# Second attention of a four-layer kernel: value packs in pairs, and one row-sum group added on DVE

## What is computed

```python
h, dh = 8, 32                                   # 8 heads of 32 channels, T = 2048
q, k, v = ...                                   # [b, h, t, dh], float32
attn = softmax(einsum('bhqd,bhkd->bhqk', q, k) * 256 ** -0.5)
attn_out = einsum('bhqk,bhkd->bqhd', attn, v)
# tokens e*512..(e+1)*512 keep only the first 256 >> e channels of attn_out:
out[:, sl, :m] = attn_out[:, sl, :m] @ o_w[:m, :m].T + o_b[:m]
```

## Time and profile before

| what | value |
|---|---|
| median of 3 executions | 5029.73 us (5026.91 to 5038.87) |
| the profiled execution | 5029.49 us |
| its span, first to last instruction | 5027.3 us, mean granted TensorE clock 0.944 |
| PE busy | 4622.3 us (92%) |
| DVE busy | 4207.0 us (84%) |
| ACT busy | 3361.4 us (67%) |
| POOL busy | 1333.6 us (27%) |

### The profile page before, as it was taken

The page is one execution under the profiler, slowest core; times in us unless marked ns, Lnnn a source line. Parts: engine busy times, 40 slices in busy tenths (PEclk is TensorE's granted clock), DMA queues, the critical chain, the costliest instruction groups (busy, mean ns, idle before and its releaser), DMA issues. The chain is left out here.

```text
span 5027.3 us, 89365 instructions
## 1 busy us (share of the span) xinstructions
PE 4622.3 (92%) x33659; PEld 2057.7 (41%) x33659; DVE 4207.0 (84%) x5551; ACT 3361.4 (67%) x6016; POOL 1333.6 (27%) x881
## 2 busy tenths in 40 slices
PE   6998775896999999999999999999998889999993
PEld 3333541563333333333333333333334445545532
DVE  6999650787999999999999999999994777777736
ACT  4888110231888888888888888888884426666663
POOL 2333210462000000000000000000001239999992
PEclk9999887996999999999999999999997769999996
DMA  5111569687333333344333333433314831323305
GB/s 188 56 55 42 186 232 394 198 271 159 43 55 50 49 49 49 50 55 55 53 49 49 49 49 54 55 55 49 49 20 153 289 86 46 82 60 79 74 5 170
DMA packets 408176, 479.48 MB, mean 95 GB/s; under 512 B 165056, under 2 KB 311264, under 8 KB 390848
## 3 DMA queue, kind: packets, MB, share of 16 engines
q1 hardware_dynamic: 394464, 455.41, 39.2%
q10 hardware_dynamic: 13280, 18.35, 1.1%
HBM read 315.71 MB, written 155.58 MB: 94 GB/s over the span
## 5 line engine op out<-in xcount | busy, mean ns | idle before, releaser
L763 DVE TENSOR_REDUCE at_NM<-at_MX 128x1 f32<-128x1024 f32 (+1 forms) x3008 | 3066.3, 1049 | 241.1 <-PE at_MX L611 216.2
L715 ACT ACTIVATE at_PB<-at_S 128x512 f32<-128x512 f32 x5056 | 2712.1, 597 | 628.3 <-PE at_S L638 503.7
L611 PE MATMUL at_MX<-at_KT,at_QT 48*128 48x512 f32 (+1 forms) x5056 | 1904.2, 454 | 60.6 <-DMA at_VS<-v 46.0
L638 PE MATMUL at_S<-at_QT,at_KT 50*128 50x512 f32 (+1 forms) x5056 | 1898.6, 441 | 8.4 <-ACT at_PB L715 6.0
L650 PE MATMUL at_AV<-at_PB,at_VS 128*32 128x256 f32 (+1 forms) x18304 | 1555.5, 414 | 0.9 <-ACT at_PB L715 0.9
L638 PEld LDWEIGHTS at_S<-at_QT,at_KT 50*128 50x128 f32 (+1 forms) x5056 | 804.8, 187 | 901.1 <-ACT at_PB L715 824.8
L611 PEld LDWEIGHTS at_MX<-at_KT,at_QT 48*128 48x128 f32 (+1 forms) x5056 | 795.8, 190 | 312.5 <-DVE at_NM L763 209.5
L650 PEld LDWEIGHTS at_AV<-at_PB,at_VS 128*32 128x32 f32 x18304 | 369.8, 108 | 820.9 <-ACT at_PB L715 752.0
L547 POOL CAST at_NMR<-at_NMF 16x128 fp32r<-16x128 f32 x79 | 22.1, 279 | 1837.5 <-ACT at_NMF L727 1837.5
L572 POOL TENSOR_TENSOR at_SUM<-at_SUM,at_PB 128x2048 f32<-128x2048 f32 x90 | 415.0, 4611 | 10.9
L913 PE MATMUL wkv_PQ<-wkv_XT,wkv_WT 128*128 128x512 f32 x768 | 340.5, 600 | 50.8 <-DVE wkv_DL L1036 34.2
(11 more groups left out here) (211 smaller groups left out, 3368.0 us busy)
## 6 DMA issues: line engine op xcount, KB each, us to landing
at_QT<-qk SPq DMA_DIRECT2D x402, 128.0 KB, 5.2
moe_W<-in_w SPq DMA_DIRECT2D x48, 1024.0 KB, 11.4
at_KT<-qk SPq DMA_DIRECT2D x384, 128.0 KB, 6.5
at_VS<-v SPq DMA_DIRECT2D x96, 256.0 KB, 9.0
at_KT<-qk SPq DMA_DIRECT2D x96, 256.0 KB, 6.3
qk<-r_HI SPq DMA_DIRECT2D x36, 512.0 KB, 4.2
qk<-r_LO SPq DMA_DIRECT2D x36, 512.0 KB, 5.2
ycat<-wkv_Y SPq DMA_DIRECT2D x32, 512.0 KB, 2.6
```

The lines of the kernel that those rows point to most:

```text
L611: ins = nc.tensor.matmul(MX[r][:, a, :], q_of(s)[h:h + NQ, b * P:(b + 1) * P], k_of(it, s, b * P // W)[h:h + NQ, (c + a) * W:(c + a + 1) * W],
L638: nc.tensor.matmul(SP_[item(it, s, "score", t)[1]][:, :], k_of(it, s, c)[h:h + NQ + 2, kb * P:(kb + 1) * P], q_of(s)[h:h + NQ + 2, c * W:( ...
L715: nc.scalar.activation(PB[:, t % NPB, :], SP_[r][:, :], ACT.Exp, scale=scale).then_inc(exp_done, 1)
L763: nc.vector.tensor_reduce(NM4[:, b, c:c + 1], MX[r][:, :, :].rearrange("p a n -> p (a n)"), AX_X, ALU.max, negate=True).then_inc(ring_got, 1)
```

## The change

Two edits in the second attention. First, the value pack of an even key block is moved to the step of the odd one behind it: `value_step(v)` uses `v | 1`, so the value packs of blocks 0 and 1 both stand after step 10, those of 2 and 3 after step 18, and so on, 8 steps apart; the L packs move with them from steps 30, 46, 54, 70, 78 to 34, 50, 58, 74, 82, and ACT's `put_sums` and DVE's `normalise` by four steps. Second, the sum of group 2 (key blocks 8 and 9) is made by DVE: `pair_sum` adds the two blocks' tiles lane by lane in four instructions of 128x512, issued behind the reductions of steps 42, 44, 46 and 48; Pool has 10 additions left. A new semaphore `pair_done` counts the four parts; the L pack of group 2 and the exponentials that overwrite key blocks 8 and 9 wait on it.

```diff
     GROUPS = () if TWO else ((0, 4), (4, 8), (8, 10), (10, 14), (14, 16))
-    NADD = NBLK - len(GROUPS)
+    ON_DVE = 2
+    NADD = sum(b - a - 1 for i, (a, b) in enumerate(GROUPS) if i != ON_DVE)
...
     def value_step(v):
 
-        return NCH * v + NCH - 1 + LAG
+        return NCH * (v if TWO else v | 1) + NCH - 1 + LAG
+
+    def group_of(kb):
+
+        return next(i for i, (a, b) in enumerate(GROUPS) if a <= kb < b)
 
     def added(kb):
 
-        i = next(i for i, (a, b) in enumerate(GROUPS) if a <= kb < b)
-        return max(kb, GROUPS[i][0] + 1) - i
+        last = max(kb, GROUPS[group_of(kb)][0] + 1)
+        return sum(max(0, min(b - 1, last) - a) for i, (a, b) in enumerate(GROUPS) if i != ON_DVE)
...
             def adds(n, s, t):
                 for i, (a, b) in enumerate(GROUPS):
-                    for kb in range(a + 1, b):
+                    for kb in range(a + 1, b if i != ON_DVE else a):
                         if NCH * (kb + 1) == t:
                             add(n, i, kb)
...
-                wait(pe, sum_done, NADD * it + added(GROUPS[i][1] - 1))
+                if i == ON_DVE:
+                    wait(pe, pair_done, NCH * (it + 1))
+                else:
+                    wait(pe, sum_done, NADD * it + added(GROUPS[i][1] - 1))
...
-                if not TWO:
+                if not TWO and group_of(old // NCH) == ON_DVE:
+                    wait(act, pair_done, NCH * (of + 1))
+                elif not TWO:
                     wait(act, sum_done, NADD * of + added(old // NCH))
...
+            def pair_sum(it, c):
+
+                a, b = (NCH * kb % NPB + c for kb in range(*GROUPS[ON_DVE]))
+                if c == 0:
+                    wait(dve, l_done, len(GROUPS) * it + ON_DVE - 1)
+                wait(dve, exp_done, NSB * it + NCH * (GROUPS[ON_DVE][1] - 1) + c + 1)
+                nc.vector.tensor_tensor(SUM[(len(GROUPS) * it + ON_DVE) % 2][:, c, :], PB[:, a, :], PB[:, b, :],
+                                        ALU.add).then_inc(pair_done, 1)
+
...
                         for unit in running(n, s, t):
                             outputs(*unit)
+                        for c in range(NCH):
+                            if t == NCH * GROUPS[ON_DVE][1] + 2 + 2 * c:
+                                pair_sum(n, c)
```

More of the change, by code:

```diff
@@ L392, in phase_attention @@
         nmf_got = m.sem("nmf_got")
-        s_put, exp_done, av_done, avs_ready, rec_done, norm_done, sum_done, l_done, ls_ready = (m.sem(n) for n in (
-            "s_put", "exp_done", "av_done", "avs_ready", "rec_done", "norm_done", "sum_done", "l_done", "ls_ready"))
+        s_put, exp_done, av_done, avs_ready, rec_done, norm_done, sum_done, pair_done, l_done, ls_ready = (
+            m.sem(n) for n in ("s_put", "exp_done", "av_done", "avs_ready", "rec_done", "norm_done", "sum_done",
+                               "pair_done", "l_done", "ls_ready"))
         sp_step, pe_step, pool_step, dve_step = (m.sem(n) for n in ("sp_step", "pe_step", "pool_step", "dve_step"))
```

## The result

The changed kernel takes 5078.03 us (median of 4 runs, 5074.08 to 5084.21), the kernel before, run beside it on the same chip, 5033.21 us (4 runs, 5026.91 to 5038.87): a ratio of 1.0091, interval 1.0077 to 1.0105. The prediction was 5066 us with a range of 5032 to 5096, and "slower" at 0.77. The medians are 44.8 us apart, where 37 were forecast. The profiled execution took 5079.6 us (span 5077.8) and that of before 5029.49 (5027.3), 50.1 us less (50.5 in span).

A forecast was written before the change was run, and what follows sets the result against it. PE's issue order was taken to set the pace; -2.6 + 2.8 + 1.0 + 1.2 + 0.4 gave +2.8 to +2.9 us a full unit, +37 us in all: 5066 us, range 5032 to 5096.

The forecast's parts named there:

- switches saved: On PE, eight of 16 value packs now stand right behind another, each saving 0.32 us: -2.6 us a unit.
- ring of three maxima: In seven of eight eight-step runs, max matmuls wait for DVE's reductions with three buffers, 0.40 us each: +2.8 us a unit.
- logarithm at step 19: ACT's Ln and Exp at the head of a run of eight delay the score of step 23: +1.0 us a unit.
- parts, all: DVE's four additions behind steps 42 to 48: +1.2 us delaying step 50's max matmul, +0.4 us for step 42's part.
- Rival 1: The three max-score buffers do not bind in runs of eight: -1.6 us a unit, 5009 us, chance 0.11.
- Rival 2: Ring costs its 0.4 us, but parts and Ln fall into existing waits: +0.6 us a unit, 5038 us, chance 0.11.
- gaps of 1 us at steps 23, 48 and 50: Signs expected on PE: 1 us before step 23's score, behind Ln and Exp, and 1 us at steps 48 and 50.
- The exclusion: A two-SBUF-input DVE part waits for a running Pool addition; step 42's part waits some 0.8 us, costing +0.4 us a unit.
- Rival 3: Pool's additions run through steps 42 to 50, every DVE part waits: about +10 us a unit, 5180 us, chance 0.08.
- Twelve units (1 to 12) are full: +34.: Twelve full units of the second attention each lose +2.8 to +2.9 us, +34 us together.
- The tail is Pool's chain: In the last unit, Pool has one addition less (-4.7 us) but starts later; 0.5 us taken.

The follow-up runs named there:

- short reductions: DVE reduces only 256 of the 512 keys of each max-score tile, against the kernel with parts in the packs: 5009.57 us in one execution.
- pairs alone: Only the value packs in pairs, all 11 additions left on Pool, against the kernel before: 5052.57 us, ratio 1.0035.
- logarithm four steps later: ACT's Ln and Exp of the row sums behind step 23 instead of 19, against the kernel with parts in the packs: 5041.42 us, 1.001 of before.
- parts alone: The changed kernel with value packs back in their old places, DVE's four parts kept: 5119.3 us, 1.017 of before.
- parts in the packs: The changed kernel with all four DVE parts behind the reduction of step 50: 5054.96 us, 1.0039 of before.
- score first: Score matmul ahead of the max matmul in the last two steps of each run of eight, against logarithm four steps later: 5116.51 us, 1.0158 of before.
- parts one and two steps earlier: Two DVE parts behind step 48 and two behind 49 instead of all behind 50, against score first: 5019.92 us, 0.9983 of before.

## Why the prediction came out as it did

**What was right: the full unit, term by term.** The forecast was a unit of about 56.2 us; it is 56.15 to 56.24, median 56.19, in eight of the twelve full units.

| Term of the sum | predicted, us a unit | measured, us a unit | by which kernels |
|---|---|---|---|
| switches saved, with the logarithm's 1.0 | -2.6 + 1.0 = -1.6 | 51.85 - 53.37 = -1.5 | short reductions, against before |
| ring of three maxima | +2.8 | 54.62 - 51.85 = +2.8 | pairs alone, against short reductions |
| logarithm at step 19, net | 1.0 - 0.4 = +0.6 | +0.70 | logarithm four steps later |
| pairs alone | +1.2 | +1.25 | pairs alone, against before |
| parts, all | +1.2 + 0.4 = +1.6 | 56.19 - 54.62 = +1.6 | changed kernel (eight units), against pairs alone |

The first two lines rest on one execution of the short reductions; its unit lengths agree within 0.3 us. That kernel has the parts in the packs too, as said above at no cost.

*The ring.* The rows showed it in advance: the wait that no row of before had could be worked out from the start-to-start times of both engines. Rival 1 (the ring does not bind) would have had 5009 us, and a kernel comes near that only when the reductions are halved. That the two agree within a microsecond is luck: the trace of this kernel has its first score 3.2 us earlier than before's (4105.4 against 4108.6), and its last unit, with more time at the lower clock, 3.1 us longer (67.2 against 64.1). Rival 2 (terms share a wait) falls, since each term is there in full, to within 0.1 us.

*The parts.* They are nearly free in the packs (+0.14) and cost 1.6 at steps 42 to 48. The traces split this further. Read at equal steps, the score matmuls of the changed kernel stand later in the unit than those of the pairs alone by the following (medians over the twelve full units):

| score of step | later by, us | the reduction that its max matmul needs |
|---|---|---|
| up to 45 | 0.01 | - |
| 47 | 0.35 | the reduction of step 44, behind part 42 |
| 48 | 0.95 | the reduction of step 45, behind part 44 as well |
| 50 | 1.56 | the reduction of step 47, behind part 46 as well |
| 60 | 1.59 | - |

The column is the sum as it was forecast: 0.35 for the part of step 42 (forecast 0.4), 0.60 and 0.61 for those of 44 and 46 (forecast 0.6 each), nothing to speak of for that of 48. Only the signs that the prediction gave were too large: it named gaps of 1 us at steps 23, 48 and 50, and PE stands idle for 0.76, 0.47 and 0.46 us there.

*The exclusion.* The forecast let a part wait for a running addition, on the earlier trace rows alone. The first part ends 0.54 us after Pool, in 1.48 us on average over the first parts of units 0 to 12 (1.23 to 1.58), where 0.68 is a free part: 0.80 longer, as forecast. Where Pool stands was right too: in unit 5 its six additions end 38.1 us into the unit (4427.27) and group 3's begins at 46.5 (4435.69), forecast 38 and 46. The page "SBUF — State Buffer" of the Trainium skill (section "Who interferes with whom") says that a DVE instruction with two SBUF inputs contends with a GpSimd instruction that reads SBUF, by an exclusive lock. The traces of the changed kernel and of four experiments (parts alone, parts in the packs, logarithm later, score first) agree with it, with parts of 5.00 us and a Pool addition of 5.11.

*Rival 3* was wrong for this kernel: in units 0 to 13 all parts but the first find Pool idle. It is a real mechanism all the same, and two of the experiments walked into it with one part in four: 1.017 and 1.016. (Its own sum is a little off: 14 units of 10 + 1.3 us give 5188 us, not 5180.)

**What was wrong: two terms, both too small.** The profiled execution is 50.5 us longer in span. By stretches of the trace: 2.5 before the first score of the second attention, 0.8 in unit 0 (forecast 1), 40.0 in the twelve full units (forecast 34), 1.5 in unit 13 (forecast 1), 4.1 in the last unit (forecast 0.5), and 1.6 behind it.

*"Twelve units (1 to 12) are full: +34."* 12 x 2.8 = 33.6 is there; the 6.4 beyond it are four units with 1.6 each. I priced the stalls at steps 48 and 50 as idle time of PE and nothing else. In units 6 to 9 the clock falls to 0.50 for 3.4 us within 1 us behind the stall of step 50, and the packs under it take 3.26 to 3.59 us instead of 1.92. Once the clock is at its full level (at 4113.1), the kernel before has no such fall until 4891.4, nor does any of the three kernels without those stalls (pairs alone, parts in the packs, logarithm later) until behind 4870.

*"The tail is Pool's chain: [...] I take 0.5."* The last unit of before is the earlier trace rows's 64.09 us, now 68.2. The timeline of PE in it, changed kernel, value packs from step 26 to step 50:

```profile
4918.18 3.33 PE L656 MATMUL at_AV<-at_PB,at_VS 128*32 128x512 f32 x16
...
4925.33 3.62 PE L656 MATMUL at_AV<-at_PB,at_VS 128*32 128x512 f32 x16
...
4938.90 3.57 PE L656 MATMUL at_AV<-at_PB,at_VS 128*32 128x512 f32 x16
```

And that of Pool:

```profile
4943.56 4.68 POOL L578 TENSOR_TENSOR at_SUM<-at_PB 128x2048 f32<-128x2048 f32 x1 [6.85 <-PE at_L L670]
```

Three of these pairs of packs run at half clock, (3.33 - 1.92) + (3.62 - 1.92) + (3.57 - 1.92) = 4.8 us more. They stand in front of the L pack of step 50 (4942.22), for which Pool waits 6.85 us, and from there Pool's chain sets the end. (DVE's four parts take 6.9 us here, from 4931.54, one of them 5.11 beside a Pool addition; the L pack that needs them comes only at 4948.70, so that costs nothing.) The unit is thus two lengths: its start to that L pack, 44.8 us, and from there to the end, 23.4. With pairs alone they are 41.5 and 24.2 us (4873.96 to 4915.50 to 4939.69), and one fall of the clock, at 4887.2, lies in the first; there Pool's additions follow each other without a break, as before, so this L pack is not what they wait for. The step that failed is thus the start of Pool's chain: "its start four steps of packs and waits later" was counted at full clock. Without the 4.8 us the last unit would be 0.7 us shorter than before's, an estimate from these numbers, where 0.5 longer was forecast.

**The expectation that failed most** ("score first") failed by the same kind of step: I priced the edit on PE, and not what a quicker PE lets in earlier. It was one L pack, which released Pool just ahead of a DVE part. The last experiment's unit came out as expected (52.4 us against 52.49 to 52.78), its whole a little below the gain expected (ratio 0.9983, expected 0.9965 to 0.998).

**Open.** Why four units of the changed kernel show a fall of the clock and eight with the same stalls don't is not settled. The length of a stall alone does not decide it: the longer stall at step 23, of 0.75 to 0.90 us, is followed by no fall in any full unit, here or with the pairs alone. Whether the stalls of steps 48 and 50 are needed together was not tried. The last unit has three falls where pairs alone have one, for no reason that the traces show. The medians are 44.8 us apart and the profiled executions 50.1, so other executions may have fewer falls; no trace of one was taken. The 2.5 us before the second attention and the 1.6 behind it were not tried.

## What to carry to other kernels

Before work is merged to save switches, look at what the switch gave time to: a burst twice as long needs a ring deep enough for the gap between producer and consumer, here 8 x (0.60 - 0.47) us against three tiles, and the loss follows from two start-to-start times of the trace before. Work added to an engine costs little in a pause of its own queue (0.14 us here for four parts) and its full time within a burst (0.6 us each), so place it by the step, not by the busy share. When a DVE addition of two SBUF tiles meets one of Pool's, the one that comes second waits to the end of the other: put a short DVE addition where Pool provably waits for something, and look again after every edit that makes another engine quicker.

## What the runs showed of the hardware

- DVE's addition with two SBUF inputs and Pool's 4.65 us addition don't overlap. A part of 0.68 us takes 5.00 us if it starts 0.22 us after Pool's has, and 5.16 at 0.05 us. In the full units of these two kernels and of the changed one, a part that meets a running addition ends 0.54 to 0.56 us after it (in one of them 0.67). The other way round Pool's takes 5.07 to 5.11 us, when it starts 0.16 to 0.18 us behind the start of a part; half a microsecond behind (parts one and two steps earlier), it keeps its 4.70 to 4.74. DVE's reductions, which read PSUM, keep their 0.68 us beside Pool (changed kernel).
- Two stalls of 0.47 and 0.46 us on PE, 1.8 us apart, were followed by 3.4 us at half the clock (1.2 of 2.4 GHz) in four of twelve units. Sixteen pack matmuls then take 3.26 to 3.62 us instead of 1.92, and the unit 1.6 us more. The single stalls of 0.75 to 0.90 us at step 23 were followed by none. Where the stall was 4.4 us long, the half clock came in every full unit, for 6.8 us in ten of twelve.
- A second value pack right behind a first costs 0.85 us (changed kernel; a value pack behind a sum pack 0.89, before), a pack alone between steps 1.20: interrupting the steps once more costs some 0.3 us, and that can be read off a trace that has both.
